# Ones matmuls over sums of four steps in part of the first attention, with a ring of ten steps of results

## The reference, cut to what matters

```python
A1 = einsum('bhqd,bhkd->bhqk', Q1, K1) * scaling      # DIM_HEAD = 16
A2 = einsum('bhqd,bhkd->bhqk', Q2, K2) * scaling
A1, A2 = where(causal, A1, -inf), where(causal, A2, -inf)
attn = softmax(A1, -1) - lam * softmax(A2, -1)
O = einsum('bhqk,bhkd->bhqd', attn, V)                # V has 32 columns
```

## Time and profile before

| what | us |
|---|---|
| median of 3 runs | 3954.69 (3953.44 to 3961.11) |
| the profiled execution, its own time | 3955.77 |
| span of the profiled execution | 3954.0 |
| PE busy in the span | 3387.4 (86%) |
| DVE busy | 2336.1 (59%) |
| POOL busy | 1703.1 (43%) |
| ACT busy | 1626.4 (41%) |

### The profile page before, as it was taken

One profiled execution on the slowest core, in us unless ns is written; L12 is line 12 of the kernel. 1 busy time (PEld: TensorE's weight loads), 2 busy tenths in 40 slices (PEclk: granted clock), 3 DMA queues, 4 the chain that ended last, 5 costly groups with the idle time before them and its releaser, 6 DMA issues. The chain is left out here.

```text
span 3954.0 us, 84812 instructions
## 1 busy us (share of the span) xinstructions
PE 3387.4 (86%) x27567; PEld 1843.8 (47%) x27567; DVE 2336.1 (59%) x5460; ACT 1626.4 (41%) x3330; POOL 1703.1 (43%) x1117
## 2 busy tenths in 40 slices
PE   6867999999999999999999985743899867984993
PEld 3322444444444444444444435643455535764662
DVE  3448777777777777777777716667211166666003
ACT  2331666666566665656566661110122133331110
POOL 1321665656565665656566663300344323220103
PEclk8986999999999999999999997855899988995997
DMA  4441111111111111111111104110433310002323
GB/s 152 153 147 44 28 48 33 46 39 39 44 34 48 38 42 43 36 45 33 48 31 47 30 11 142 44 44 0 130 80 79 54 41 15 1 0 87 106 95 96
DMA packets 229278, 224.88 MB, mean 57 GB/s; under 512 B 88721, under 2 KB 198546, under 8 KB 222738
## 3 DMA queue, kind: packets, MB, share of 16 engines
q1 hardware_dynamic: 213522, 194.34, 16.6%
q0 software_dynamic: 15360, 25.44, 3.3%
HBM read 138.58 MB, written 80.35 MB: 55 GB/s over the span
## 5 line engine op out<-in xcount | busy, mean ns | idle before, releaser
L637 POOL TENSOR_TENSOR attention_probs<-attention_probs 128x1024 f32<-128x1024 f32 (+2 forms) x640 | 1228.3, 1919 | 869.0 <-PE attention_ps_o L774 869.0
L667 ACT ACTIVATE attention_probs<-attention_ps_s 128x512 f32<-128x512 f32 (+3 forms) x2560 | 1197.8, 538 | 838.0 <-PE attention_ps_s L749 466.3
L697 DVE TENSOR_REDUCE attention_chunk_max<-attention_ps_m 128x1 f32<-128x512 f32 x1536 | 1005.4, 686 | 247.5 <-PE attention_ps_m L795 245.5
L795 PE MATMUL attention_ps_m<-attention_k_stack,attention_q_stack 96*128 96x512 bf16 (+3 forms) x2560 | 878.4, 358 | 43.0 <-DMA attention_v_head<-v_rows 33.7
L745 PE MATMUL attention_ps_s<-attention_q_stack,attention_k_stack 99*128 99x512 bf16 (+3 forms) x2560 | 798.6, 351 | 40.1 <-issue 27.0
L774 PE MATMUL attention_ps_o<-attention_probs,attention_v_head 128*32 128x256 f32 (+1 forms) x9728 | 640.6, 366 | 1.0 <-issue 0.6
L693 DVE CUSTOM_DVE_ANT_0 attention_ps_m<-attention_ps_m,attention_mask_wide 128x128 f32<-128x128 f32 (+3 forms) x1024 | 500.1, 498 | 219.0 <-PE attention_ps_m L795 201.5
L795 PEld LDWEIGHTS attention_ps_m<-attention_k_stack,attention_q_stack 96*128 96x128 bf16 x2560 | 243.7, 97 | 458.4 <-DVE attention_chunk_max L697 183.8
L785 PE MATMUL attention_ps_o<-attention_probs,consts 128*32 128x256 f32 (+1 forms) x5120 | 415.4, 360 | 0.4 <-POOL attention_probs L637 0.4
L774 PEld LDWEIGHTS attention_ps_o<-attention_probs,attention_v_head 128*32 128x32 f32 x9728 | 264.4, 109 | 273.6 <-issue 111.6
L745 PEld LDWEIGHTS attention_ps_s<-attention_q_stack,attention_k_stack 99*128 99x128 bf16 x2560 | 247.7, 98 | 305.4 <-ACT attention_probs L667 144.1
(11 more groups left out here) (278 smaller groups left out, 3632.7 us busy)
## 6 DMA issues: line engine op xcount, KB each, us to landing
qk_parts<-project_parts SPq DMA_DIRECT2D x64, 384.0 KB, 3.0
heads_out<-attention_results_sb SPq DMA_DIRECT2D x256, 64.0 KB
out_heads<-heads_out SPq DMA_DIRECT2D x8, 2048.0 KB, 8.0
experts_w<-in_f_w SPq DMA_DIRECT2D x16, 1024.0 KB, 8.4
attention_q_stack<-qk_parts SPq DMA_DIRECT2D x32, 384.0 KB
attention_k_stack<-qk_parts SPq DMA_DIRECT2D x32, 384.0 KB
experts_w<-in_e_w SPq DMA_DIRECT2D x24, 512.0 KB, 4.8
v_rows<-project_v SPq DMA_DIRECT2D x8, 1024.0 KB, 4.0
```

The source lines that it names most:

```text
L637: pool.tensor_tensor(probs[:, to, :, lo:], probs[:, to, :, lo:], probs[:, k % RING_P, :, lo:], ALU.add).then_inc(pair_ok, 1)
L667: act.activation(probs[:, k % RING_P, a, left(k):], ps_s[(2 * k + a) % RING_S][:, left(k):], ACT.Exp, scale=float(DH) ** -0.5).then_inc(pr ...
L697: last = dve.tensor_reduce(to, ps_m[m % RING_M][:, 0:w], AX.X, ALU.max)
L795: pe.matmul(ps_m[m % RING_M][:, 0:w], qs[at][0:STACK, a, jq * P:(jq + 1) * P], ks[at][0:STACK, a, c * GROUP:c * GROUP + w], start=True, st ...
```

## The change

The sums of steps 24 to 35 (the twelve full steps of the last turn) are now taken by four steps. POOL adds steps 24 and 25, then 26 and 27, and then, behind a wait for its own second add, the one pair to the other (L648 of the changed kernel), counting `four_ok`; so for 28 to 31 and for 32 to 35. The ones matmuls use the sum of four. All other steps are summed by pairs as before. The ring of results has ten steps instead of eight. A head has 17 groups of ones instead of 20, and POOL 23 adds instead of 20.

`ONES_AT` says in which iteration a group of ones stands: a pair's at its first step + 2, as before, and a four's at its first step + 6. So the sums of 24, 28 and 32 are used in the iterations k = 30, 34 and 38, and the pair of 36 at 38 too.

```diff
-PAIR = 2
+PAIR, QUAD = 2, 4
+
+FOURS = range(len(STEPS) - GT * Q_TILES, len(STEPS) - GT, QUAD)
+SUMS = [(k, QUAD if k in FOURS else PAIR) for k in range(0, len(STEPS), PAIR) if k - PAIR not in FOURS]
...
-        RING_P, RING_S, RING_M, RING_O, RING_R = 8, 3, 3, 2, 4
+        RING_P, RING_S, RING_M, RING_O, RING_R = 10, 3, 3, 2, 4
...
+        ONES_AT = [k + count + (PAIR if count == QUAD else 0) for k, count in SUMS]
...
                         pool.tensor_tensor(probs[:, to, :, lo:], probs[:, to, :, lo:], probs[:, k % RING_P, :, lo:],
                                            ALU.add).then_inc(pair_ok, 1)
+                        if k + 1 - QUAD in FOURS:
+                            pool.wait_ge(pair_ok, head.n * PAIRS + (k + 1) // PAIR)
+                            four = (k + 1 - QUAD) % RING_P
+                            pool.tensor_tensor(probs[:, four], probs[:, four], probs[:, to], ALU.add).then_inc(four_ok, 1)
...
-                        if k % PAIR == 0 and a == 0:
-
-                            act.wait_ge(ones_ok, head * PAIRS + k // PAIR + 1)
+                        old = (k - RING_P) % N_STEPS
+                        if old in FIRST and a == 0:
+
+                            act.wait_ge(ones_ok, head * N_SUMS + FIRST[old] + 1 + (N_SUMS if k >= RING_P else 0))
...
-                pe.wait_ge(pair_ok, head * PAIRS + pair + 1)
+                if count == QUAD:
+                    pe.wait_ge(four_ok, head * len(FOURS) + FOURS.index(k) + 1)
+                else:
+                    pe.wait_ge(pair_ok, head * PAIRS + k // PAIR + 1)
...
-                    if k > 0:
-                        ones(head, k // PAIR - 1)
-                    elif not is_first(head):
-                        ones(head - 1, PAIRS - 1)
+                    for n in range(N_SUMS):
+                        if ONES_AT[n] == k:
+                            ones(head, n)
+                        elif ONES_AT[n] == k + N_STEPS and not is_first(head):
+                            ones(head - 1, n)
```

More of the change, by code:

```diff
@@ L516, in attention0 @@
         ps_o = [s.ps(f"ps_o{i}", [P, 2, BLOCKS, P]) for i in range(RING_O)]
-        names = ("ready", "score_ok", "prob_ok", "values_ok", "pair_ok", "ones_ok", "max_ok", "max_used", "steps",
+        names = ("ready", "score_ok", "prob_ok", "values_ok", "pair_ok", "four_ok", "ones_ok", "max_ok", "max_used", "steps",
                  "neg_ok", "parts_ok", "parts_in", "taken")
-        (ready, score_ok, prob_ok, values_ok, pair_ok, ones_ok, max_ok, max_used, steps, neg_ok, parts_ok,
+        (ready, score_ok, prob_ok, values_ok, pair_ok, four_ok, ones_ok, max_ok, max_used, steps, neg_ok, parts_ok,
          parts_in, taken) = (s.sem(n) for n in names)
@@ L525, in attention0 @@
         LOADS = len(RUNS[0]) + len(RUNS[1]) + 1
-        PAIRS = N_STEPS // PAIR
+        PAIRS, N_SUMS = N_STEPS // PAIR, len(SUMS)
+        FIRST = {k: n for n, (k, _) in enumerate(SUMS)}
+        ONES_AT = [k + count + (PAIR if count == QUAD else 0) for k, count in SUMS]
         STORES = 2 * 2
@@ L650, in take @@
                 act.wait_ge(values_ok, head * N_STEPS + LAST[turn] + 1)
-                act.wait_ge(ones_ok, head * PAIRS + (LAST[turn] + 1) // PAIR + RING_P // PAIR)
+                act.wait_ge(ones_ok, head * N_SUMS + FIRST[LAST[turn] - 1] + 1 + N_SUMS)
                 act.activation(results[:, slot], ps_o[turn % RING_O][:], ACT.Copy).then_inc(taken, 1)
@@ L728, in _ @@
         def _(pe):
-            pe.sem_inc(ones_ok, RING_P // PAIR)
+            pe.sem_inc(ones_ok, N_SUMS)
             pe.wait_ge(ready, 1)
@@ L776, in values, with ones @@
                 last.then_inc(values_ok, 1)
-            def ones(head, pair):
-                k = pair * PAIR
+            def ones(head, n):
+                k, count = SUMS[n]
                 turn, tq, kb = STEPS[k]
                 psum = ps_o[turn % RING_O]
-                pe.wait_ge(pair_ok, head * PAIRS + pair + 1)
+                if count == QUAD:
+                    pe.wait_ge(four_ok, head * len(FOURS) + FOURS.index(k) + 1)
+                else:
+                    pe.wait_ge(pair_ok, head * PAIRS + k // PAIR + 1)
                 for strip, half, a, block in strips(k):
@@ L853, in step @@
                 if after is None:
-                    ones(head, PAIRS - 1)
+                    ones(head, N_SUMS - 1)
             run(pe, step)
```

## The result

The changed kernel takes 4065.97 us (median of 6 runs, 4057.33 to 4069.0), the kernel before 3957.27 us beside it (6 runs). The ratio is 1.0272, 95% interval 1.0258 to 1.0286: slower by 2.7%, 108 us. The forecast was 4065.

What follows compares the result with a forecast made beforehand. PE was taken as issue-bound, with POOL short of room in the last turn. From 3954.7 us, 84 for PE's waits on POOL, net of saved ones, and 26 for the clock gave 4065; range 4025 to 4105.

Steps and rivals of the forecast that it cites:

- What bounds the kernel: First attention: PE is issue-bound; three fewer groups of ones at 0.445 us save 1.34 us per head.
- POOL does not keep up: Last turn: POOL needs 7.2 us per four steps; PE stands 3.99 us, so a head gets 2.54 us longer.
- forecast without overlaps: POOL's queue in the last turn, adds at full 2.36 us: head 2.65 us longer; with overlaps 2.41.
- What would show it: Trace signs: gapless POOL from add 27 to 39, PE waits at k = 34 and 38, heads 63.7 us or more.
- The last heads: End of the stage: the last head, without maxima in its last turn, takes 5 us more.
- The clock: Behind PE's stands at k = 38: a fall costs 1.7 us, 53 us over 31 heads; half taken, 26.
- The ring, DVE and ACT: Ring of ten costs nothing, its waits met by PE's order; DVE and ACT idle time can't shorten POOL's wait.
- POOL keeps up: Rival: POOL's adds come in time, all 43 us are saved, 3912 us; chance 0.04.
- the clock holds: Rival: POOL is late in the last turn but the clock does not fall, 4039 us; chance 0.18.
- the clock falls each time: Rival: the clock falls in every head, 4092 us, up to 4110 if a fall costs more; chance 0.13.
- the forecast's own break-even: POOL's last-turn queue: with a full add below 2.03 us instead of 2.36 the head is not longer.

Runs made afterwards that it cites:

- The filled stand: Changed kernel with eight more 512-column matmuls on PE ahead of the ones of iteration 38: 4037.41 us, 1.0188 to the kernel before.
- the run of the adds alone: Kernel before with three more full POOL adds per head, behind steps 27, 31 and 35, into an unread spare tile: 4052.08 us, ratio 1.0236.

## Why the prediction was right

**What bounds the kernel.** Right. With PE's groups alone taken out, the head lost 1.29 us of the 1.34 worked out from the distance of starts, and not the 8.6 that durations added up would give.

**POOL does not keep up.** Right, in place and order. With the clock of the changed trace set 504.80 us ahead (1736.50 for 1231.70), the forecasts and the measured starts are:

| | forecast | measured |
|---|---|---|
| sum of 24 | 1742.00 | 1742.01 |
| sum of 28 | 1749.16 | 1749.08 |
| sum of 32 | 1756.32 | 1756.14 |
| ones of 32 | 1758.73 | 1758.54 |
| ones of the pair of 36 | 1760.54 | 1760.30 |

The table is of the forecast without overlaps; with 0.05 us of overlap at each add that does not wait, its last row would be 1760.29. So the head's price was at the low end of what I gave, 2.41 and not the 2.54 in the middle: 31 x 0.13 = 4 us too much. ("What would show it" asked for 63.7 us or more a head; the six heads without a fall take 63.6.)

**The last heads.** Half right. I charged one head without maxima in its last turn with 5 us. The last head did take 5 us more: from its first add to the last ones of the stage 19.65 us before and 24.84 after. But the maxima of the last turn are those of the head after next, so the last two heads have none there: in the profiled executions the last of the 31 distances, that of the head before the last, went from 53.27 to 59.10 us, 5.8 more where I had counted 2.54. That is 3 us too little, and it nearly cancels the term above.

**The clock.** I took half of 53 us, 26. In the profiled executions the 15 falls make the 21 heads 30 us longer than 21 x 63.60. The eight heads with a pause go the other way: they take 38 us more than eight others, and took 45 before, so 7 us come back there, which I had not counted. That leaves 23 us. With the waits the attention's sum is then 29 heads x 2.42, 8.3 for the last two distances and 5.2 for the last head, 84 us, and 23 on top, 107 in all; I had 84 and 26. The filled stand gives 29 to 33 us for the falls alone. So both terms came out near, but the 26 was only half way between two ends, 0 and 53, and that it lies so near is luck.

**The ring, DVE and ACT.** Right: 1.0005 for the ring, and PE's waits for ACT and DVE are as small as before (4.1 us for exp).

**Rivals.** "POOL keeps up" is out, "the clock holds" and "the clock falls each time" were both wrong as they stood; it falls in 15 heads of 21. On the forecast's own break-even, a full add under 2.03 us, nothing ran; all 480 full adds stayed at 2.34 to 2.38 us in the changed kernel.

What is left open: which stands make the clock fall and which don't. It is not their length or their place in the head. Counted from the first add of the last turn, the three waits of PE start at the same times and last equally long, both to 0.03 us, in the six heads without a fall and in 13 of the 15 with one; in the other two only the last wait is shorter (0.71 and 0.89 us for 1.13), and there the clock had fallen before it.

## What to carry to other kernels

Moving work off the bound engine onto one with 39% idle time pays only if that engine has the room in the same turn: count its queue item by item between two points where it is idle, not over the stage. An in-order engine that takes its sums from another one should ask for them as late as its buffers allow; the same instructions gave +2.7% with the ones early and all in one turn, -0.2% with two groups one iteration later, and -1.1% with the adds spread over two turns and the ones later. The stand of PE of some 3 us, broken by one group, cost up to 2.7 us more in clock here, and three waits of about 1 us apart from each other cost nothing more than themselves; where a producer has to be late, it is worth trying to spread its lateness over several short waits.

## What the runs showed of the hardware

- An add of 128 x 1024 f32 with both inputs in SBUF took DVE 1.44 to 2.31 us beside POOL's adds in 90 cases of 96 (3.36 in two, 1.22 or 1.23 in four). The last one of the stage had no POOL add beside it and took 1.23:

```profile
2418.18 1.23 DVE L734 TENSOR_TENSOR attention_probs<-attention_probs 128x1024 f32<-128x1024 f32 x1 [2.24 <-POOL attention_probs L643]
```

- POOL's adds that started while DVE was adding went from 2.35 to 2.56 and 2.84 us, and the small one from 0.72 to 1.31 us. Those that had run for 1 us or more when a DVE add began kept their 2.35 or 2.36, also where the two then ran side by side for over 1 us. In the kernel before, where DVE's maxima read PSUM (L693 with one more input in SBUF), all of POOL's full adds in the stage took 2.34 to 2.36 us. The Trainium skill ("GPSIMD Engine Reference", Specifications) says that GpSimd's SBUF interfaces are shared with VectorE and that they contend with VectorE instructions that have two SBUF inputs. The trace agrees, and shows both engines slower.
- An add on POOL that waits for the add before it starts 0.08 us after its end (1744.32 + 4.68 to 1749.08 in the changed kernel); with a second wait in front of it, 0.16 us (in the run of the adds alone).
- Eight matmuls more in a stand of each head made the program 33 us faster by the ratios: the granted clock stayed at 1.00 in the 21 heads away from the pauses.
